# Experts' gate and up products from split rows and split weights in an attention and mixture-of-experts block

## The reference

```python
buf = jnp.zeros((E, CAP + 1, Hq), x.dtype).at[sorted_e, dest].set(x[tok])
g = jnp.einsum('ech,ehf->ecf', buf, w_gate)
u = jnp.einsum('ech,ehf->ecf', buf, w_up)
y = jnp.einsum('ecf,efh->ech', jax.nn.silu(g) * u, w_down)
out = jnp.zeros((T, Hq), x.dtype).at[tok].add(gath * wv[:, None])
sh = jax.nn.silu(x @ sw_gate) * (x @ sw_up) @ sw_down
```

## Time and profile before

| | us |
|---|---|
| median of 3 runs (765.27 to 766.3) | 765.53 |
| profiled execution | 769.37 |
| its span, first to last instruction | 766.9 |
| TensorE busy | 731.1 (95%) |
| VectorE busy | 531.6 (69%) |
| ScalarE busy | 467.7 (61%) |
| POOL busy | 425.5 (55%) |

### The profile page before, as it was taken

The page is one execution under the profiler, slowest core; times in us unless marked ns, Lnnn a source line. Parts: engine busy times, 40 slices in busy tenths (PEclk is TensorE's granted clock), DMA queues, the critical chain, the costliest instruction groups (busy, mean ns, idle before and its releaser), DMA issues.

```text
span 766.9 us, 12813 instructions
## 1 busy us (share of the span) xinstructions
PE 731.1 (95%) x4114; PEld 620.8 (81%) x4114; DVE 531.6 (69%) x1552; ACT 467.7 (61%) x1277; POOL 425.5 (55%) x337
## 2 busy tenths in 40 slices
PE   3899999999999999999999999999988999999997
PEld 3688889998899898889989888989866767777775
DVE  4598788679877768987776797778665215564373
ACT  5688878777886677788667777877554212222110
POOL 0644445554466488646647875654534517468356
PEclk9999999999999999999999999999999999999999
DMA  8960005800005011100401101040359689996772
GB/s 294 322 136 1 2 1 175 287 1 2 1 1 168 26 40 48 40 1 1 158 8 40 46 28 62 16 165 1 123 145 237 191 289 272 282 240 74 163 233 82
DMA packets 62353, 84.42 MB, mean 110 GB/s; under 512 B 6312, under 2 KB 50229, under 8 KB 62288
## 3 DMA queue, kind: packets, MB, share of 16 engines
q1 hardware_dynamic: 51440, 70.56, 29.8%
q0 software_dynamic: 7680, 8.95, 6.2%
q10 hardware_dynamic: 3168, 4.11, 1.5%
HBM read 54.81 MB, written 33.51 MB: 115 GB/s over the span
## 4 chain that ended last, share of the span: by engine, by line
PE 76%; DVE 11%; ACT 6%; DMA 2%; issue 2%; POOL 1%; SPq 0%; ACTq 0%; POOLq 0%
PE PJ L1335 22%; PE OUT L1443 9%; PE U L1428 6%; PE U L1388 6%; PE U L1593 5%; PE U L1417 4%; PE U L1387 3%; PE U L1429 3%; PE U L1335 3%; PE OUT L1539 3%; PE U L1539 2%; PE XB L1612 2%; PE OUT L1612 2%; PE XB L1335 2%; ACT U L546 1%
## 5 line engine op out<-in xcount | busy, mean ns | idle before, releaser
L768 POOL TENSOR_TENSOR qsw<-qsw,sinT 128x512 f32<-128x512 f32 x96 | 126.2, 1314 | 184.6 <-ACT qsw L533 183.7
L977 DVE CUSTOM_DVE_ANT_0 U<-U,mask 128x128 f32<-128x128 f32 (+1 forms) x256 | 86.6, 379 | 54.8 <-PE U L1388 54.4
L546 ACT ACTIVATE U<-U,nmax 128x128 f32<-128x128 f32 (+1 forms) x256 | 100.4, 392 | 32.2 <-DVE nmax L977 31.7
L1335 PE MATMUL PJ<-hT_hi,w_hi 128*128 128x512 f32 x256 | 113.8, 445 | 4.0 <-DVE hT_lo L951 3.7
L1335 PE MATMUL PJ<-hT_lo,w_hi 128*128 128x512 f32 x256 | 103.5, 404 | 0.0
L1335 PE MATMUL PJ<-hT_hi,w_lo 128*128 128x512 f32 x256 | 103.1, 403 | 0.0
L772 POOL TENSOR_TENSOR qr<-qr,qsw 128x512 f32<-128x512 f32 x64 | 82.5, 1289 | 31.3 <-DVE qr L965 30.8
L532 ACT ACTIVATE qsw<-PJ 64x512 f32<-64x512 f32 x96 | 57.0, 594 | 58.1 <-PE PJ L1335 49.3
L779 POOL DMA_INDIRECT slot_rows<-xn,sidx x64 | 64.4, 1006 | 45.6 <-issue 12.0
L1443 PE MATMUL OUT<-wo_hi,oT_hi 128*128 128x256 f32 x256 | 83.0, 324 | 1.4 <-DVE wo_lo L1001 1.2
L994 DVE TENSOR_TENSOR oT_lo<-U,oT_hi 128x256 fp32r<-128x256 f32 x128 | 54.1, 423 | 41.2 <-ACT oT_hi L553 41.0
(11 more groups left out here) (212 smaller groups left out, 1827.6 us busy)
## 6 DMA issues: line engine op xcount, KB each, us to landing
wgu<-in_dram SPq DMA_DIRECT2D x32, 352.0 KB, 9.4
expert_sum<-blank SPq DMA_DIRECT2D x3, 2176.0 KB, 17.8
slot_rows<-blank SPq DMA_DIRECT2D x1, 4624.0 KB, 26.3
late_sums<-expert_sum SPq DMA_DIRECT2D x9, 512.0 KB, 8.9
wd_a<-in_dram SPq DMA_DIRECT2D x12, 352.0 KB
wraw<-in_dram SPq DMA_DIRECT2D x8, 512.0 KB, 11.5
bcm<-mod_rows SPq DMA_DIRECT2D x8, 512.0 KB, 6.8
xe<-slot_rows ACTq DMA_DIRECT2D x10, 289.0 KB, 6.3
```

The lines of the kernel that those rows point to most:

```text
L546: last = act.activation(U[n % 3][:, a:z], U[n % 3][:, a:z], ACT.Exp, scale=-1.0, bias=nmax[:, n % 4, j:j + 1], accum_out=rsum[:, n % 4, j: ...
L768: pool.tensor_tensor(pair3(qsw[:, n % NQSW, :]), pair3(qsw[:, n % NQSW, :]), both(sinT[:, :]), ALU.mult).then_inc(t2_done, 1)
L977: last = dve.tensor_tensor_reduce(out=U[n % 3][:, a:z], in0=U[n % 3][:, a:z], in1=allowed, scale=-float(HD) ** -0.5, scalar=3.4e38, op0=AL ...
L1335: last = pe.matmul(out_ap, a(c), b_(c), start=(n == 0), stop=(n == len(steps) - 1))
```

## The change

The experts' gate and up become six short-format products: high and low part of the transposed rows with high and low part of the weights, without low by low. ScalarE writes the high parts (`xeT_hi` from the bank, `wgu_hi` from the ring, in a ring of three experts), VectorE subtracts to get the low parts; `wgu_lo` lies where the weights themselves lie, and `xeT_lo` where the cosine and sine tables were. The weights of expert n+1 are split in slot n, so both engines get a slot -1. The wait for the weights' load moves from TensorE to ScalarE.

```diff
--- before.py
+++ after.py
@@ -43,7 +43,7 @@
 W_FREE = NU - UNITS // 2
 SW_PARTS = 4
 SWC = 2 * FS // SW_PARTS
-NSUM = 3
+NSUM, NGU = 3, 3
 ROW = H + E + 1
 TOKEN = H + E
 NQSW, NOT = 3, 3
@@ -69,8 +69,11 @@
         xnt_d = nc.dram_tensor("xn_transposed", [NPAIR, PN, 2, HC, TOK], F32, kind="Internal").ap()
 
 
-        cosT = sb("cosT", [PN, S])
-        sinT = sb("sinT", [PN, S])
+        tables = ExitStack()
+        cosT = sb("cosT", [PN, S], F32, tables)
+        sinT = sb("sinT", [PN, S], F32, tables)
+        tables.close()
+        xeT_lo = sb("xeT_lo", [PN, 2, H], F32R)
         mask = sb("mask", [PN, 2 * PN])
         ident = sb("ident", [PN, PN])
         tri = sb("tri", [PN, PN])
@@ -176,10 +179,14 @@
         sw_stack.close()
         sw_lo = sb("sw_lo", [PN, HC, 2 * FS], F32R, exps)
         rings = ExitStack()
-        wgu = sb("wgu", [PN, RING, 2, HC, F], F32, rings)
+        gu_raw = ExitStack()
+        wgu = sb("wgu", [PN, RING, 2, HC, F], F32, gu_raw)
+        gu_raw.close()
+        wgu_lo = sb("wgu_lo", [PN, RING, 2, HC, F], F32R, rings)
         wd_a = sb("wd_a", [FH, WD_A, 2, H], F32, rings)
         slot_w = sb("slot_w", [PN, E], F32, rings)
         slot_token = sb("slot_token", [PN, E], I32, rings)
+        wgu_hi = sb("wgu_hi", [PN, NGU, 2, HC, F], F32R, rings)
         rings.close()
 
         late_sums = sb("late_sums", [PN, NPAIR - 1, NSUM, TT, H], F32, exps)
@@ -200,7 +207,7 @@
         first_sums = sb("first_sums", [PN, NSUM, TT, H], F32, sums_at)
         sums_at.close()
         xe = sb("xe", [PN, RING, ROW])
-        xeT = sb("xeT", [PN, 2, H])
+        xeT_hi = sb("xeT_hi", [PN, 2, H], F32R)
         sgl = sb("sgl", [PN, 2, F])
         hh = sb("hh", [PN, 2, F])
         hhT = sb("hhT", [FH, 2, 2 * PN])
@@ -264,6 +271,7 @@
         ld_gu = [sem(f"ld_gu{i}") for i in range(HALF)]
         ld_wd = [sem(f"ld_wd{i}") for i in range(HALF)]
         ld_xe = [sem(f"ld_xe{i}") for i in range(HALF)]
+        gu_hi_done, gu_lo_done, xe_hi_done = sem("gu_hi_done"), sem("gu_lo_done"), sem("xe_hi_done")
         xe_ps, xe_done, told, gu_ps, sgl_done, hh_done, hh_ps, hht_done, ye_ps, ye_done = (
             sem(n) for n in ("xe_ps", "xe_done", "told", "gu_ps", "sgl_done", "hh_done", "hh_ps", "hht_done", "ye_ps", "ye_done"))
         ld_sw, ld_swd, ld_gb = sem("ld_sw"), sem("ld_swd"), sem("ld_gb")
@@ -695,6 +703,18 @@
 
             def expert_slot(n):
 
+                if 0 <= n < E:
+                    act.wait_ge(xe_ps, n + 1)
+                    if n >= 2:
+                        act.wait_ge(gu_ps, n - 1)
+                    act.activation(xeT_hi[:, n % 2, :], PJ[n % 2][:, 0:H], ACT.Copy).then_inc(xe_hi_done, 1)
+                if n + 1 < E:
+                    e = n + 1
+                    if e % 2 == 0:
+                        act.wait_ge(ld_gu[e % RING // 2], 32 * (e // RING + 1))
+                    if e >= NGU:
+                        act.wait_ge(gu_ps, e - NGU + 1)
+                    act.activation(wgu_hi[:, e % NGU, :, :, :], wgu[:, e % RING, :, :, :], ACT.Copy).then_inc(gu_hi_done, 1)
                 if 0 <= n - 1 < E:
                     act.wait_ge(gu_ps, n)
                     if n - 1 >= 2:
@@ -705,7 +725,7 @@
                     if n - 2 >= 2:
                         act.wait_ge(ye_ps, n - 3)
                     act.activation(hhT[:, (n - 2) % 2, :], PT[(n - 2) % 2][0:FH, 0:2 * PN], ACT.Copy).then_inc(hht_done, 1)
-                if n % 2 == 1 and n - 1 + RING < E:
+                if n > 0 and n % 2 == 1 and n - 1 + RING < E:
                     e = n - 1 + RING
                     i = (e // 2) % HALF
                     act.wait_ge(xe_ps, e + 2 - RING)
@@ -734,7 +754,7 @@
                 silu_of(1, f)
             for t in range(TT):
                 shared_rows(1, t)
-            for n in range(E + 3):
+            for n in range(-1, E + 3):
                 expert_slot(n)
             for q in range(2, NPAIR):
                 for f in range(FT):
@@ -1246,12 +1266,11 @@
                 hidden(1, f)
 
             def expert_slot(n):
-                if n < E:
-
-                    dve.wait_ge(xe_ps, n + 1)
-                    if n >= 2:
-                        dve.wait_ge(gu_ps, n - 1)
-                    dve.tensor_copy(xeT[:, n % 2, :], PJ[n % 2][:, 0:H]).then_inc(xe_done, 1)
+                if 0 <= n < E:
+
+                    dve.wait_ge(xe_hi_done, n + 1)
+                    dve.tensor_tensor(xeT_lo[:, n % 2, :], PJ[n % 2][:, 0:H], xeT_hi[:, n % 2, :].bitcast(F32),
+                                      ALU.subtract).then_inc(xe_done, 1)
                     if n % 2 == 0:
 
                         i = n % RING
@@ -1267,6 +1286,11 @@
                         dve.wait_ge(hh_ps, n - 2)
                     dve.tensor_tensor(hh[:, (n - 1) % 2, :], SC[(n - 1) % 2][:, F:2 * F], sgl[:, (n - 1) % 2, :],
                                       ALU.mult).then_inc(hh_done, 1)
+                if n + 1 < E:
+                    e = n + 1
+                    dve.wait_ge(gu_hi_done, e + 1)
+                    dve.tensor_tensor(wgu_lo[:, e % RING, :, :, :], wgu[:, e % RING, :, :, :],
+                                      wgu_hi[:, e % NGU, :, :, :].bitcast(F32), ALU.subtract).then_inc(gu_lo_done, 1)
                 if 0 <= n - 3 < E:
                     e = n - 3
                     dve.wait_ge(ye_ps, e + 1)
@@ -1585,13 +1609,12 @@
                 if 0 <= n - 1 < E:
                     e, i = n - 1, (n - 1) % RING
                     pe.wait_ge(xe_done, e + 1)
-                    if e % 2 == 0:
-                        pe.wait_ge(ld_gu[i // 2], 32 * (e // RING + 1))
+                    pe.wait_ge(gu_lo_done, e + 1)
                     if e >= 2:
                         pe.wait_ge(hh_done, e - 1)
-                    for c in range(HC):
-                        last = pe.matmul(SC[e % 2][:, 0:2 * F].rearrange("p (g f) -> p g f", g=2), xeT[:, e % 2, c * PN:(c + 1) * PN], wgu[:, i, :, c, :],
-                                         start=(c == 0), stop=(c == HC - 1))
+                    last = halves(SC[e % 2][:, 0:2 * F].rearrange("p (g f) -> p g f", g=2), HC,
+                                  ((lambda c: xeT_hi[:, e % 2, c * PN:(c + 1) * PN], lambda c: xeT_lo[:, e % 2, c * PN:(c + 1) * PN]),
+                                   (lambda c: wgu_hi[:, e % NGU, :, c, :], lambda c: wgu_lo[:, i, :, c, :])))
                     last.then_inc(gu_ps, 1)
                 if 0 <= n - 2 < E:
                     e = n - 2
```

## The result

The changed kernel took 768.1 us (764.94 to 771.13 over its runs), the kernel before 764.88 (762.36 to 770.32) beside it. The ratio of the runs is 1.0035 with an interval of 1.0019 to 1.0051: **slower by 0.35%, some 2.7 us** (the two medians lie 3.2 us apart, the two means 2.8). The profiled execution took 767.83 us for a span of 766.0. Totals scatter by 3 us, and part of it arises before the experts (the shared products ahead of them ended at 623.0, 621.1, 621.5 and 625.6 in four profiles). So all that follows is read from the first gate and up product on: 624.00 here, 625.48 in the earlier trace rows's profile. I call these distances "on the stage's clock".

What follows compares the result with a forecast made beforehand. Two chains end within half a microsecond: TensorE's, and the one through scatters, sums and POOL. Sums late by 1.6 + 0.5 + 0.6 = 2.7, less 0.3 slack, give +2.4: 765.5 + 2.4 = 767.9 us, range 763.2 to 770.8.

Steps and rivals of the forecast that it cites:

- lock meetings: Expert stage: new VectorE subtraction and POOL take turns by whole instructions, making the sums late; end +2.4 us, chance 0.47.
- the next thing that is late is the sums: After the experts: TensorE's 5.3 us gain goes nowhere, as VectorE stands at the first combine until the scattered sums land.
- 2 x 0.8: Two gating spells: a subtraction goes between POOL's two operations and costs POOL about 0.8 each time, 1.6 us.
- clearly slower: Rival: VectorE becomes the bound of the expert stage, time about 773; two slower cases have 0.06 together.
- four stalls of 1.5: VectorE in the expert stage: stalls behind the gating operations, half an operation each, add 6 us.
- 2.6 us slot: VectorE per expert: with 0.45 of waiting a slot costs 2.6 instead of 2.50, 3 us in all.
- d: How much later the sums come: 2.7 us forecast; the end moves by about d - 0.3.
- the 1.1 I had: Scatters meeting subtractions: 0.5 us for those behind the spells (experts 5, 13), 0.6 for six more.
- 0.4 for the rows': Stage start: the rows' split puts a ScalarE step before VectorE's, 0 to 0.80 us once, taken as 0.4.
- if that wait were gone: Stage start: without TensorE's wait for gathered rows, splitting expert 0's weights would cost 0.80 + 0.88 us; taken as no cost.
- Transfers decide: Rival, scatters: buffers freed sooner end weight loads up to 4.5 us earlier, scatters land quicker; -2.1 us, 763.4, chance 0.19.
- six products cost 1.41: Rival, TensorE gate and up: slot 2.7 us, end 7 us later, about 773; two slower cases have 0.06 together.

Runs made afterwards that it cites:

- experiment 4: Changed kernel with both gating spells behind the last scatter and the weight loads of experts 12 to 31 left out; ratio 1.0012 to the kernel before.
- the halves: Changed kernel with each POOL operation of 128x1024, in gating and combines, made as two of 128x512, nothing moved; ratio 1.0056 to the kernel before.

## Why the prediction was right in the number and half right in the way

**The size and sign.** Forecast +2.4 us and 767.9; measured 2.7 and 768.1. The case it stands for, lock meetings between the new subtraction and POOL, is shown as what costs the time: with the gating spells out of the way the ratio is 0.9969, and without the subtraction's size 0.9998. The way to the number was another than forecast, so that it came out within 0.3 us is luck.

**The step that failed** is the one by which TensorE leaves the experts near 701.3 and, of the time it gains there, the prediction says "the next thing that is late is the sums". The product price was right (six records 0.16 apart, 0.96 to 0.97 us), but TensorE left at 706.38. I had POOL pay for the meetings in the spells and VectorE for none; the trace shows the reverse. Of the four gating operations one was longer (2.91 against 2.35, +0.56; in the second spell none), where I had 2 x 0.8. Inside the stage TensorE waited 5.2 us, which put the experts' starts back by 6.4, and half clock by 1.6 more: 8.0 of the 8.1 us by which the change's experts (82.4) exceed the run with the gating last (74.3). This was the mechanism I had under "clearly slower" ("four stalls of 1.5"), which I gave one chance together with a 2.6 us slot that didn't come. Together they are more than the 7 us that the products gave, and in the profiles TensorE is 1.3 (each kernel's first profile) to 2.3 us late (means of two), so the stalls belonged beside the forecast and not at 773. The trace of the kernel before had the warning: VectorE's copy held up for 2.25 and 2.46 us behind the gating.

**The sums** did come late, as a term: on the stage's clock the last scatter stood at 90.7 and 88.1 before, 91.2 and 91.9 after, so d = 2.2 in the means against 2.7, with 2.6 us between the two of the kernel before. Its parts were other ones: the spells gave 0.6 instead of 1.6, the scatters (sum of their lengths up 2.9 and 5.2 us) more than the 1.1 I had, partly hidden in transfer waits. Scatters of expert 5 and 13 were due at or after 650.6 and 678.2; they came at 649.64 and 676.53, which on the stage's clock is 25.6 (25.1 and 24.0 before) and 52.5 (52.7 and 51.2 before). VectorE's wait for the first sums was to be 6 us or more; it was 0.73, because both chains were late together. What late sums alone would have cost the end, no run tells.

**The last stage** I took as unchanged. TensorE needed 1.4 us more there, twice, from a combine of VectorE that now starts behind POOL's (3.43 and 3.42 us against 1.22 in both profiles of the kernel before). The run with the low part left out has it too (3.43), so it does not hang on the weights' subtraction. The loads of the sums landed for POOL 16.1 us after their first issue (719.13 to 735.21) instead of 17.5 (720.07 in the earlier trace rows to 737.60); what shortened them by 1.5 us no run tells. Against this stands the end: 3.2 instead of 4.8 us after TensorE, which cancels it.

**The start.** I had 0 for the weights' split and 0.4 for the rows'. When the gathered rows are there in time, the split of expert 0's weights is on the chain (the rows from 622.01 to 624.00): 2.5 us to the first product against 1.0. That was the case "if that wait were gone", and both profiles of the change show it. The clock of the first products comes on top: 1.4 us against a start at full clock, a term that I had not got.

**The rivals.** "Transfers decide" had the mechanism (experiment 4: scatters follow TensorE without loads) but it did not act here, as TensorE freed no buffer sooner. The price "six products cost 1.41" is refuted. That the weights' wait on ScalarE would cost 1 us shows in no row.

## What to carry to other kernels

Before giving VectorE an instruction with two operands in SBUF inside a pipelined stage, list every POOL instruction of that stage and charge each meeting to both: to POOL's chain the VectorE instruction, and to whatever waits behind VectorE's queue the whole POOL instruction, which can be longer by a factor of three (here 2.35 to 2.94 us against 0.88). What such a wait costs depends on the room in VectorE's slot: the same gating cost TensorE nothing before the change. Move long POOL work to where VectorE is idle before adding such an instruction: here the same change lost 0.35% with the gating inside the stage and gained 0.31% with it behind. And when two engines combine at the end, moving their inputs earlier can cost more than it brings.

## What the runs showed of the hardware that I had not expected

- The wait is for the whole instruction of the other engine, whatever the own size: a 128x8 subtraction took 2.72 and 2.18 us, a copy of 128x2 took 3.20, behind POOL operations of 2.4 to 2.9. That the copy, with one input, is held too was not in my sum, though the kernel before shows it (2.25 and 2.46 us). The Trainium skill (SBUF — State Buffer, section Who interferes with whom) counts copies among the operations that can take the shared port pair, and the trace agrees.
- An indirect transfer's issue is lengthened by a subtraction: from 1.55 to between 1.69 and 2.2 us. With equal periods this locks in step, nine times 2.18 to 2.20; with a slot of 2.28 us nine scatters took 1.69 to 2.03. With the subtraction cut to 8 columns none of the 32 took over 1.60. The same section says that a VectorE tensor_tensor, unlike a copy, was not seen to hold up the transfers that GpSimd issues. Here the measurement decides against it: the scatter is back at 1.56 once the last subtraction is over.
- The clock: after TensorE's wait of 2.01 us ending at 677.91 the six products took 1.71 instead of 0.96 us, and the granted clock was 0.89 over the stretch 670 to 685. In the first spell, with waits of 1.41 and 0.61 us, it stayed at 1.00 over 640 to 655. In the changed kernel with the gating last it was 1.00 through 640 to 700.
- What stays open: why runs of one kernel differ by 3 us and more, why the sums' loads land 1.5 us sooner in the change, and why the scatters were 4 us late with the halves, of which the longer spells are 1 and 1.8 were there before them.
